# Running one mixture-of-experts layer by sorted token blocks instead of densely

## The reference

```python
# layer 2 ("L1"): attention with 16 heads over 32 context keys, then 8 experts, two per token
x = x + tanh(g_xattn[1]) * L1_attention(layernorm(x), ctx)
xn = layernorm(x)
probs = softmax(xn @ router_w.T)                       # 8 experts
topk_probs, topk_idx = top_k(probs, 2); topk_probs /= topk_probs.sum(-1)
h = gelu_new(einsum('nc,ech->neh', xn, w_fc) + b_fc)   # 128 -> 512, every expert
out = einsum('neh,ehc->nec', h, w_proj) + b_proj       # 512 -> 128
x = x + tanh(g_ffn[1]) * sum_over_chosen(out * topk_probs)
# layer 3 ("L2"): a circular convolution along the 512 tokens, by Fourier transforms
y = irfft(rfft(layernorm(x), axis=1) * rfft(weight * k_mod, n=512), axis=1)
x = x + tanh(g_xattn[2]) * y
x = x + tanh(g_ffn[2]) * L2_moe(layernorm(x))          # 32 experts of 64, 4 per token
# layer 4 ("L3"): attention, then a shared part and 16 experts, two per token
```

## Time and profile before

| | us |
|---|---|
| median of 3 runs | 1008.73 |
| lowest, highest | 1004.59, 1011.96 |
| profiled execution, its span | 994.9, 993.1 |
| mean granted TensorE clock | 0.973 of full |

### The profile page before, as it was taken

One profiled execution on the slowest core, in us unless ns is written; L12 is line 12 of the kernel. 1 busy time (PEld: TensorE's weight loads), 2 busy tenths in 40 slices (PEclk: granted clock), 3 DMA queues, 4 the chain that ended last, 5 costly groups with the idle time before them and its releaser, 6 DMA issues.

```text
span 993.1 us, 13719 instructions
## 1 busy us (share of the span) xinstructions
PE 866.9 (87%) x4007; PEld 593.8 (60%) x4007; DVE 654.7 (66%) x1807; ACT 476.5 (48%) x905; POOL 473.7 (48%) x425
## 2 busy tenths in 40 slices
PE   3899969898989699799989999989998988797885
PEld 2377846666666366566766766656554554455663
DVE  4256678889898577557776675878677754453554
ACT  0034324544445333467757667665665656322331
POOL 2000015656567343265576656546544666253662
PEclk9999979999999979999999999999999999899998
DMA  4012305252520000200000000023000000012324
GB/s 121 1 43 54 98 1 193 82 202 86 187 79 11 0 1 1 64 11 1 12 6 6 12 0 6 1 58 105 1 0 1 12 15 11 9 36 67 98 61 128
DMA packets 62002, 46.70 MB, mean 47 GB/s; under 512 B 20691, under 2 KB 57954, under 8 KB 61800
## 3 DMA queue, kind: packets, MB, share of 16 engines
q1 hardware_dynamic: 56688, 41.21, 14.0%
q0 software_dynamic: 2528, 4.27, 1.3%
q10 hardware_dynamic: 2712, 0.33, 0.2%
HBM read 22.03 MB, written 24.74 MB: 47 GB/s over the span
## 4 chain that ended last, share of the span: by engine, by line
PE 56%; DVE 23%; issue 7%; POOL 6%; ACT 4%; ACTq 1%; DMA 1%; SPq 1%; DVEq 0%; POOLq 0%
PE psum L1113 50%; DVE hb L2107 2%; POOL h_lo L640 2%; DVE xn L1763 2%; DVE hb L2108 1%; DVE hb L2101 1%; PE psum L1504 1%; ACTq L784 1%; POOL s L686 1%; POOL rstd L598 1%; DVE mr L1859 1%; ACT h_hi L873 1%; PE psum L1185 1%; DVE stats L1750 1%; DVE hb L2105 1%
## 5 line engine op out<-in xcount | busy, mean ns | idle before, releaser
L640 POOL TENSOR_TENSOR h_lo<-hb,h_hi 128x512 fp32r<-128x512 f32 x164 | 210.8, 1290 | 216.6 <-ACT h_hi L873 215.1
L873 ACT ACTIVATE h_hi<-hb 128x512 fp32r<-128x512 f32 x196 | 122.7, 626 | 76.4 <-DVE hb L2108 51.7
L1113 PE MATMUL psum<-xt_hi,wa_hi 128*128 128x512 f32 x272 | 127.4, 468 | 17.9 <-DVE hb L2108 14.0
L2101 DVE TENSOR_TENSOR hb<-hb,psum 128x512 f32<-128x512 f32 x128 | 86.9, 685 | 60.3 <-ACT hb L852 55.4
L855 ACT ACTIVATE hb<-psum 128x512 f32<-128x512 f32 x136 | 80.8, 594 | 67.1 <-PE psum L1113 67.0
L852 ACT ACTIVATE hb<-psum,bfc 128x512 f32<-128x512 f32 x128 | 87.6, 685 | 52.0 <-PE psum L1113 50.9
L1113 PE MATMUL psum<-xt_lo,wa_hi 128*128 128x512 f32 x272 | 107.4, 395 | 0.0
L635 POOL TENSOR_TENSOR hb<-hb,wsb 128x512 f32<-128x512 f32 x64 | 82.1, 1283 | 49.0 <-DVE hb L2105 44.5
L1113 PEld LDWEIGHTS psum<-xt_hi,wa_hi 128*128 128x128 f32 x272 | 51.8, 190 | 41.8 <-DVE hb L2108 21.6
L598 POOL TENSOR_TENSOR rstd<-veps,neghalf 128x4 f32<-128x4 f32 x24 | 24.2, 1009 | 104.9 <-DVE veps L1755 104.1
L2105 DVE TENSOR_TENSOR hb<-hb,psum 128x512 f32<-128x512 f32 x68 | 46.0, 684 | 41.1 <-ACT hb L855 28.1
(11 more groups left out here) (371 smaller groups left out, 1989.5 us busy)
## 6 DMA issues: line engine op xcount, KB each, us to landing
s<-l_lo SPq DMA_DIRECT2D x13, 1386.0 KB, 6.9
xn<-s SPq DMA_DIRECT2D x47, 66.0 KB, 1.9
stage<-in_L_ffn_w_fc SPq DMA_DIRECT2D x8, 256.0 KB, 3.0
stage<-in_L_ffn_w_proj SPq DMA_DIRECT2D x8, 256.0 KB, 3.1
stage<-in_L_ffn_W SPq DMA_DIRECT2D x12, 128.0 KB, 2.4
const<-in_consts SPq DMA_DIRECT2D x1, 1152.0 KB, 6.6
x<-in_x SPq DMA_DIRECT2D x4, 256.0 KB, 3.4
stage<-in_L_ffn_expert_gate SPq DMA_DIRECT2D x4, 256.0 KB, 3.4
```

The lines of the kernel that those rows point to most:

```text
L640: pool.tensor_tensor(h_lo[:, k % 3, :], hb[:, k % 4, :], h_hi[:, k % 3, :].bitcast(F32), ALU.subtract).then_inc(q["hlo_pool"], 1)
L873: act.activation(h_hi[:, k % 3, :], hb[:, k % 4, :], ACT.Copy).then_inc(q["hhi_done"], 1)
L1113: return pe.matmul(o, l, r, start=start, stop=stop, skip_group_check=True)
L2101: dve.tensor_tensor(h, h, W[(k // 4) % 2][:, :], ALU.mult).then_inc(q["h_done"], 1)
```

## The change

Layer 2's feed-forward takes the sorted form. Each token is written twice, by expert, to a memory s1 of 138 x 128 rows, and 39 blocks of 128 rows are run (4096 rows make 32 full blocks, and 7 more for the partly filled last ones). A block uses plain float32 matmuls: 1 transpose, 4 up products and 4 down products, each 128 x 128 x 128. The up weights, biases and output bias of a block's expert come with one DMA of 128 x 644 numbers per block into one of 6 slots. The down weights of all experts lie in SBUF (`wpr`).

Its routing moves into the attention: steps 5, 9, 13 and 16 start batches 0 to 3 (`D1_BASE`), so that batch 3's and part of batch 2's runs after the attention's 16 steps. The layer 3 spectrum is made beside it. The transforms of batches 0 and 1 and the routing of layer 3's batch 0 follow the blocks, and batches 2 and 3 are transformed in layer 3's feed-forward. The weights of layer 3 are now copied in the attention.

```diff
-ROUTED = [16, 32, 16, 16]
+ROUTED = [16, 0, 16, 16]
+NB1 = 2 * B * S // 128 + E1 - 1
+WS = 6
+D1 = dict(mom=0, scl=0, xt=1, logits=2, shift=3, exp=3, top=4, cum=4, slots=5, scatter=6)
+D1_BASE = [5, 9, 13, 16]
+COUNT1_PE = [21, 22, 23]
+TAP1, SPEC1 = 17, 19
-XE = 15
-XL = 8
+XE = 12
+XL = 6
...
             sp.wait_ge(q["tabi_done"], 1)
             sp.wait_ge(d_scat, 16 * 8 * B)
-            for j in range(NB3):
+            for j in range(NB1):
...
+                row = sp.value_load(tabi[0:1, 128 + j:129 + j], min_val=1, max_val=ROWS1 - 128)
+                sp.dma_start(xe3[:, j % XE, :], s1[bass.ds(row, 128), :]).then_inc(d_xe[j % XL], 16)
+                if j >= WS:
+                    sp.wait_ge(q["ye3_done"], j - WS + 1)
+                e = sp.value_load(tabi[0:1, j:j + 1], min_val=0, max_val=E1 - 1)
+                sp.dma_start(w1s[j % WS], a["pack1"][bass.ds(e, 1), :, :].rearrange("a p n -> p (a n)")).then_inc(d_w1[j % WS], 16)
...
+            def dispatch(n, j):
...
+                pool.indirect_dma_start(s1, bass.IndirectOffsetOnAxis(idx3[:, n, i, k:k + 1], 0),
+                                        xs3[i][:, TB * n + k, :], None).then_inc(d_scat, 16)
...
+                    if 0 <= t - D1["scatter"] < TB:
+                        dispatch(n, 2 * (t - D1["scatter"]))
+                        dispatch(n, 2 * (t - D1["scatter"]) + 1)
...
+            def gelu1(j):
+                act.wait_ge(q["up1_ps"], j + 1)
...
+                for c in range(4):
+                    last = act.activation(hb[:, j % 3, 128 * c:128 * c + 128], G[j % 2][:, 128 * c:128 * c + 128],
+                                          ACT.Gelu_apprx_tanh, bias=w1s[j % WS][:, F1 + c:F1 + c + 1])
...
+            def up1(j):
+                pe.wait_ge(q["xet_sb"], j + 1)
+                pe.wait_ge(d_w1[j % WS], 16 * (j // WS + 1))
...
+                for c in range(4):
+                    last = mm(G[j % 2][:, 128 * c:128 * c + 128], w1s[j % WS][:, 128 * c:128 * c + 128], xe1t[:, j % 2, :], True, True)
...
+            def down1(j):
+                pe.wait_ge(q["ge1_done"], j + 1)
...
+                    for i in range(NB1 + 2):
+                        if i < NB1:
+                            experts1[i] = pe.value_load(tabi[0:1, i:i + 1], min_val=0, max_val=E1 - 1)
+                            rows_t1(i)
+                        if 0 <= i - 1 < NB1:
+                            up1(i - 1)
+                        if 0 <= i - 2 < NB1:
+                            down1(i - 2)
+                    transform(0)
+                    inverse(0)
+                    transform(1)
+                    xt_in(5, 0)
+                    logits(2, 0)
+                    inverse(1)
+                    running(0)
+                    comb_in(2, 0)
...
+            def result1(j):
+                dve.wait_ge(q["dn3_ps"], j + 1)
+                r = xe3[:, j % XE, 0:128]
+                link(dve.tensor_tensor(r, (U[1], ACC)[j % 2][:, 0:128], w1s[j % WS][:, F1 + 4:PACK1], ALU.add))
+                dve.tensor_scalar(r, r, xe3[:, j % XE, 129:130], None, ALU.mult).then_inc(q["ye3_done"], 1)
```

More of the change, by code:

```diff
@@ L37 @@
 CAPACITY = 2 * 512 * 4 // 32
[L38 removed]
+UB = CB[0:4]
 E3, F3 = 16, 128
@@ L119, in moe3_constants, with pack_layer1 @@
     return c
+def pack_layer1(w_fc, b_fc, b_proj):
+    c = np.zeros((E1, 128, PACK1), np.float32)
+    c[:, :, 0:F1] = w_fc
+    c[:, :, F1:F1 + 4] = np.reshape(b_fc, (E1, 4, 128)).transpose(0, 2, 1)
+    c[:, :, F1 + 4:PACK1] = np.reshape(b_proj, (E1, 1, 128))
+    return c
 class Chain:
@@ new lines, in rows_in1, with logits1 @@
+            def rows_in1(n):
+                pe.wait_ge(q["c_ln"], n + 1)
+                use_t()
+                for k in range(TB):
+                    last = pe.transpose(T[:, 128 * k:128 * k + 128], xs3[0][:, TB * n + k, 0:128], ident)
+                last.then_inc(q["c_xt"], 1)
+            def logits1(n):
+                use_t()
+                for k in range(TB):
+                    last = mm(T[:, E1 * k:E1 * k + E1], x3t[n % 3][:, 128 * k:128 * k + 128], rw1[:, :], True, True)
+                last.then_inc(q["d_lg"], 1)
@@ new lines, in down1, with block_counts @@
+            def down1(j):
+                pe.wait_ge(q["ge1_done"], j + 1)
+                if j >= 2:
+                    pe.wait_ge(q["ye3_done"], j - 1)
+                for c in range(4):
+                    last = mm((U[1], ACC)[j % 2][:, 0:128], hb[:, j % 3, 128 * c:128 * c + 128],
+                              wpr[:, bass.ds(experts1[j], 1), c, :].rearrange("p a n -> p (a n)"), c == 0, c == 3)
+                last.then_inc(q["dn3_ps"], 1)
+            experts1 = {}
+            def block_counts(part, done, sel, E):
@@ new lines, in chain1 @@
+            def chain1(g):
+                for n in reversed(range(B)):
+                    t = g - D1_BASE[n]
+                    if t == D1["mom"]:
+                        moments3(n)
+                    if t == D1["shift"]:
+                        shift_route1(n)
+                    if t == D1["top"]:
+                        choose_route1(n)
+                    if t == D1["slots"]:
+                        slots(n, 0, E1)
+                        if n == B - 1:
+                            block_table(0, E1)
```

819 lines of the change are left out of this document (401 added, 418 removed).

## The result

The changed kernel takes **953.58 us** (951.67 to 958.75, 4 runs), the one before 1006.66 (1001.68 to 1011.96, 4 runs): ratio 0.948, 95% interval 0.9416 to 0.9544. The forecast was 947 in a range of 922 to 982. The profiled execution took 952.83, with a span of 951.0.

The account below looks back on a forecast made before the run. PE bounds the kernel, busy 87% of the span, and layer 2's dense feed-forward is its longest stage. The terms sum to -62.0 us, taken from the median 1008.7 for 947, in a range of 922 to 982.

Parts of the forecast that it names:

- The exchange (L to layer 3): From L, the attention's last product, to layer 3's first: 255.8 us go, head, steps, drain and tail come, -72.5 together.
- the head: From L to the first up product: +40.7 us, POOL's 22 scatters ending last, bounds 34 and 50.
- The 38 steps: Layer 2's 39 blocks: 38 steps of 2.4 us, +91.2, PE, SP and PE's sequencer near each other; 76 to 106.
- Drain and tail: Last block to the first add, +10.4 us; from there to layer 3's first expert product, +41.
- The first (pitch 2.1): Rival in the blocks: PE bounds them and the head is tight, pitch 2.1, 932 us; chance 0.15.
- The second (the bytes): Rival in the blocks: the weight fetch bounds them, pitch 3.1 (+27), 974 us; chance 0.17.
- The third (the low clock in the blocks): Rival: the blocks run at 1.2 GHz, pitch 4.5 (+80), 1027 us, slower than before; chance 0.05.
- The attention, +8: Attention: 3.3 us for 30 added PE records, 4.7 for six bank T waits, POOL and DVE covered; 0 to 20.
- The start, -1.5: Start: four bias loads leave ACT's chain, -1.5 us; POOL's new wait for the row marks is covered.
- Layer 1's feed-forward, no term: Layer 1's feed-forward: the prediction gave no term, counted as 0.
- Layer 3, +4: Layer 3's feed-forward: two transforms and inverses instead of one on PE, 2 x 1.95 us; bounds 0 and 10.
- Layer 4, 0: Layer 4's blocks: fewer slots (6 and 12 for 8 and 15) cost 0, since six ahead cover the way.

Follow-up runs that it names:

- the split kernel: The changed kernel with the weights of every odd block issued by ACT instead of SP: 948.22 us, ratio 0.9402.
- the half weights: The changed kernel, fetching only half of each expert's packed weights from the seventh block on: 949.97 us, ratio 0.9424.
- ring 12: The kernel before with 12 slots of rows and a lead of 6 blocks in layer 4, for its 15 and 8: 1006.68 us, ratio 1.0003.
- the stand-ins: The changed kernel with 16 ACT copies and 16 POOL differences, results unread, where layer 1's feed-forward held layer 2's weight splits: 956.51 us, ratio 0.9492.
- the warm tail: The changed kernel with 112 unread filler products on PE between the last block and layer 3's first expert product: 944.52 us, ratio 0.9407.
- the first try: The changed kernel with 175 unread filler products on PE between the last block and layer 3's first expert product: 950.47 us, ratio 0.9448.

## Why the prediction was right, and where it was not

**The exchange (L to layer 3): right.** -70.6 for -72.5. That it is this near is in part luck, since the two largest misses, 4.0 in the head and 3.9 in the steps, cancel. Replacing a PE-bound dense stage whose ends could both be read left only the new stage to build, and layer 4's rows gave its steps. The head was 4.0 too short: the last scatter came 1.9 later than forecast (one of its waits, 3.75, behind the spectrum's products at the low clock), the rows landed 5.6 after it for 5.2, and the first up product stands in PE's row behind the second block's transpose, whose rows SP loads one turn later. The 38 steps are 3.9 too long: I had put 0.1 of jitter on top of the largest of three. The largest was SP, put at 2.3 and measured at 2.3 (2.27 for an undisturbed pair), and PE's own 2.2 shows at 2.2 once SP is relieved (blocks of 2.0 and 2.2 in turn, a few longer). PE's sequencer (2.3) was no bound: in the split kernel PE starts its blocks without "issue". And PE's idle time was put down mostly to the rows' DMA, 5.7 us, only 1.4 to "issue". Drain and tail: 53.2 for 51.4, with the clock and the ping-pong between DVE and PE as described.

**The rivals.** The first (pitch 2.1) fell by SP. The second (the bytes) fell by the half weights. The third (the low clock in the blocks) fell too: 1.00 from 480 to 547. PE waits only 7.7 us there, at most 2.2 at once, beside 59.2 of work. The Trainium skill's rule ("TensorE: Matmul & The Clock Gate", section "HAM oscillation — how this bites in real kernels") is for a loop in which the wait for a DMA is longer than the burst of matmuls before it. The blocks aren't such a loop, so their 1.00 doesn't speak against the page; the rival had taken the rule too wide. The trace agrees with it where PE is starved for long (head 0.58, tail 0.56). At the attention's end the clock fell to 0.50 after 10 us in which PE was busy 4.8 (395 to 405). The prediction read a fall at the head of layer 4's blocks too; in the kernel before the clock stands at 1.00 there (875 to 901).

**The attention, +8: the step that failed most in what the change does.** It measured +13.4. The sum had 3.3 for PE's added records, which is what they took, and 4.7 for six waits at bank T, of which the trace shows two of 0.78 and perhaps one of 0.7. The gaps grew by 6.2 all the same, and 4.2 of it stands behind DVE (the softmax's sum and the choice of experts), which I had called covered because it had 27 idle us of 82: idle time on average is no cover for steps that stand in an engine's row ahead of a link of the path. The clock, 3.8, had no term. The place where it falls moves between executions of the same kernel: 81.0, 81.0 and 87.9 in three profiles of before and its twin with ring 12. The changed attention took 94.3 to 98.1 in eleven profiles. So a part of the 13.4 may differ in the next execution.

**The start, -1.5: wrong in sign, +2.3.** "Covered, since PE reaches its first own work long after" was the failed step: POOL's next work behind the marks was the first link of PE's. The question to ask was what is queued behind the wait on POOL.

**Layer 1's feed-forward, no term: -6.9.** The change removes work from there (the splits for layer 2), and I followed only PE's. PE was idle 17 us of this stretch, and DVE, for which it waits, was slowed by its neighbours; the stand-ins gave back 5.1 of the 6.9. This miss hides the start's and half of the attention's.

**Layer 3, +4: measured +8.1.** The 32 added records are the 4. About 2 are the cold start, as the warm tail shows (187.0); the other 2 were not followed.

**Layer 4, 0: not settled by the two profiles.** The sum was made against an execution that stood 13.8 below the median, and I took that difference over. Ring 12's execution, at 1009.1 and the same median as before, shows where such a difference can lie: 14.2 us above the first profile, 6.9 of it in the attention (87.9 for 81.0) and 7.3 in layer 4's blocks (73.5 for 66.2). After's profile holds both, in the attention and in the blocks. That is why the span's forecast missed by 20 us (931 for 951) and the median's by 6.6 (947 for 953.6). Taking the difference over came out near by luck: the 20 us that the span's forecast missed and the 13.8 that were added mostly cancel, since after's execution already stands at its median.

## What to carry to other kernels

Cost a stage that is exchanged from the nearest relative's rows, then walk through every other stage for what the change adds or takes on engines that are not the bound there: a neighbour's work on PE's supplier here was worth 5 us of a stretch, and small steps queued ahead of a link of the path cost more than their length. Before a difference of 10 us between two profiles is explained, profile the kernel before a second time. Where a block loop's loads take their address from a register, count issues per block before bytes, and share them between two engines.

## What was not expected of the hardware

- DVE's same 359 instructions took 157.7 us beside 16 + 16 splits on ACT and POOL, 148.0 without, 154.9 with them put back.
- Loads by register, undisturbed, start 1.1 to 1.2 us apart on SP, for the 66 KB of rows as for the 330 KB of weights.
- Idle products that only keep PE busy gave back 7 us of a 50 us tail (clock 0.56 to 1.00) and 2 in the stage behind it, but only 3 in the first try, with 63 more of them, 39 of these at one place.
- SP's pauses of about 0.7 us without a shown wait, 0 to 15.2 us together in layer 4's blocks, differ between executions of one kernel.
- While POOL issued 22 scatters in a row, PE's last small sums stood 1.4 to 2.8 us apart with no wait shown, and cost 5.5 us at the end.
